# Decoder kernel on one core: the second cross attention's maxima are split behind their turning, and the expert layer's first weights are loaded and split under the attention's end

## Reference

```python
# layer 1 cross attention: 16 batches, 16 heads of 8 channels, 56 queries, 1500 keys
qh = _split_heads(q @ W_q.T + b_q, bs)
kh = _split_heads(k @ W_k.T + b_k, bs)
vh = _split_heads(v @ W_v.T + b_v, bs)
scores = jnp.einsum('bhqd,bhkd->bhqk', qh, kh) / jnp.sqrt(jnp.float32(D_K))
weight = jax.nn.softmax(scores, axis=-1)
attn = jnp.einsum('bhqk,bhkd->bqhd', weight, vh)
x = x + attn.reshape(...) @ W_o.T + b_o
# layer 1 experts: all 8 experts on all 896 tokens
gate = jax.nn.softmax(x @ Wg + bg, axis=-1)          # less a learned threshold, clipped, normalised
h = jax.nn.gelu(jnp.einsum('td,edf->etf', x, W1) + b1[:, None, :])
eo = jnp.einsum('etf,efd->etd', h, W2) + b2[:, None, :]
out = jnp.einsum('te,etd->td', w, eo)
```

## Time and profile before

| | |
|---|---|
| median of 3 runs | 1433.26 us (1430.25 to 1434.88) |
| profiled execution, its own time | 1429.79 us |
| its span in the trace | 1428.0 us |
| busy: PE / DVE / ACT / POOL | 1356.4 / 1065.1 / 864.0 / 767.4 us |

### The profile page before, as it was taken

One profiled execution on the slowest core, in us unless ns is written; L12 is line 12 of the kernel. 1 busy time (PEld: TensorE's weight loads), 2 busy tenths in 40 slices (PEclk: granted clock), 3 DMA queues, 4 the chain that ended last, 5 costly groups with the idle time before them and its releaser, 6 DMA issues.

```text
span 1428.0 us, 25410 instructions
## 1 busy us (share of the span) xinstructions
PE 1356.4 (95%) x9220; PEld 1012.2 (71%) x9220; DVE 1065.1 (75%) x2128; ACT 864.0 (61%) x1849; POOL 767.4 (54%) x431
## 2 busy tenths in 40 slices
PE   7889999999999999999998987899999999999898
PEld 4648888888888888888866754555556556555687
DVE  6458778888777887778844677677777777776787
ACT  4437667666667666667623553566666666665575
POOL 5026443334444444442260291588888888885363
PEclk9899999999999999999999999999999999999999
DMA  3132222211212222221150123446446446420331
GB/s 85 61 91 52 57 57 57 55 43 36 49 52 58 57 51 57 57 57 36 43 151 15 57 64 80 115 104 139 106 101 138 110 95 139 94 66 1 87 105 45
DMA packets 71803, 104.39 MB, mean 73 GB/s; under 512 B 14670, under 2 KB 54934, under 8 KB 71550
## 3 DMA queue, kind: packets, MB, share of 16 engines
q1 hardware_dynamic: 60062, 91.39, 25.6%
q10 hardware_dynamic: 11616, 11.38, 3.0%
HBM read 63.65 MB, written 2.11 MB: 46 GB/s over the span
## 4 chain that ended last, share of the span: by engine, by line
PE 79%; DVE 11%; DMA 3%; ACT 2%; issue 2%; SPq 1%; POOL 1%; ACTq 0%; DVEq 0%; POOLq 0%
PE PS L701 9%; PE PS L1104 6%; PE PS L715 6%; PE PS L689 5%; PE PS L690 5%; PE PS L691 5%; PE PS L1118 5%; PE PS L717 5%; PE PS L716 5%; PE PS L1084 5%; PE PS L1043 3%; PE PS L1049 3%; DMA inv_kept<-row_inv 2%; PE PS L744 2%; DVE QO_area L1399 2%
## 5 line engine op out<-in xcount | busy, mean ns | idle before, releaser
L1233 POOL TENSOR_TENSOR QO_area<-QO_area,prob_a 125x896 f32<-125x896 f32 x150 | 315.1, 2101 | 22.7 <-ACT prob_a L1325 3.2
L867 ACT ACTIVATE HL<-PS 125x512 fp32r<-125x512 f32 (+1 forms) x384 | 206.8, 539 | 177.8 <-PE PS L701 160.7
L959 DVE TENSOR_TENSOR HL<-PS,HL 125x512 fp32r<-125x512 f32 (+1 forms) x384 | 238.0, 622 | 74.6 <-ACT HL L867 53.5
L1399 DVE TENSOR_REDUCE QO_area<-PS 112x1 f32<-112x500 f32 x384 | 238.9, 670 | 60.3 <-PE PS L1084 60.2
L1325 ACT ACTIVATE prob_a<-PS 125x448 f32<-125x448 f32 x384 | 187.5, 540 | 103.9 <-PE PS L1104 100.5
L774 POOL TENSOR_TENSOR HL<-ctx_area,ones 125x512 fp32r<-125x512 f32 (+1 forms) x64 | 93.1, 1454 | 247.3 <-PE PS L717 189.3
L715 PE MATMUL PS<-HL 125*128 125x512 f32 (+1 forms) x384 | 155.7, 405 | 2.4 <-DVE HL L959 2.0
L689 PE MATMUL PS<-HL 128*128 128x500 f32 x336 | 153.1, 456 | 4.7 <-DVE HL L929 3.9
L1104 PEld LDWEIGHTS PS<-HL 98*125 98x125 f32 x768 | 102.9, 186 | 71.4 <-ACT prob_a L1325 37.9
L877 ACT ACTIVATE prob_a<-prob_a,neg_max 128x500 f32<-128x500 f32 x192 | 135.5, 706 | 26.7 <-DVE neg_max L951 25.4
L1084 PE MATMUL PS<-HL 96*112 96x500 f32 x384 | 129.4, 408 | 17.9 <-DVE QO_area L1399 15.3
(11 more groups left out here) (262 smaller groups left out, 2743.3 us busy)
## 6 DMA issues: line engine op xcount, KB each, us to landing
HL<-prob_b SPq DMA_DIRECT2D x128, 187.5 KB, 4.0
ctx_area<-in_ctx_T SPq DMA_DIRECT2D x16, 750.0 KB, 13.4
ctx_area<-in_ctx SPq DMA_DIRECT2D x16, 750.0 KB
HL<-ctx_area SPq DMA_DIRECT2D x64, 187.5 KB, 3.8
inv_area<-in_ctx_T SPq DMA_DIRECT2D x8, 750.0 KB, 4.1
prob_a<-in_ctx_T SPq DMA_DIRECT2D x8, 750.0 KB, 4.7
inv_area<-inv_kept ACTq DMA_DIRECT2D x16, 256.0 KB, 3.5
ctx_area<-in_L_ffn_W SPq DMA_DIRECT2D x16, 256.0 KB, 3.4
```

The costliest lines, as they stand in the source:

```text
L867: nc.scalar.activation(pH[k % 3][0:KC, 0:width(g)], PS[0:KC, 2 + k % 3, 0:width(g)], ACT.Copy)\
L959: nc.vector.tensor_tensor(pL[k % 3][0:KC, 0:width(g)], PS[0:KC, 2 + k % 3, 0:width(g)], pH[k % 3][0:KC, 0:width(g)].bitcast(fp32), ALU.sub ...
L1233: nc.gpsimd.tensor_tensor(late_acc[b % 2], before, late_p[n % LATE_P], ALU.add).then_inc(m["padd"], 1)
L1399: nc.vector.tensor_reduce(late_part[b % 2][:, u // NKB, u % NKB:u % NKB + 1], PS[0:2 * S, u % NKB, 0:KB], AX, ALU.max).then_inc(m["mx"], 1)
```

## The change

The maxima are turned over first, eight columns of plain fp32, and split afterwards: ScalarE's copy out of PSUM bank 7 rounds them to the high row, VectorE subtracts that from the same PSUM bank for the low row (`low_maxima`, signal `nmlow`). The turning and ScalarE's copy move from step 1 to step 0 of the batch; the low row's DMA is issued in step 1, behind a wait for `nmlow`. Batch b+2's first keys wait for `nmlow` in place of `nmcopy`.

In the expert layer SP's first loads wait for the last stack, and GpSimd's splitting waits for the last add of the probabilities, in place of the residual. The split weights get another place in `HL`: behind the first of the three key stacks, where the second was.

```diff
-        hl_taken = [0]
-        xn_hl = [halved(128, NTOK) for i in range(2)]
+        hl_taken = [4 * S2]
         w1_hl = [[halved(128, FF) for h in range(2)] for i in range(2)]
         w2_hl = [[halved(128, FF) for h in range(2)] for i in range(2)]
+        xn_hl = [halved(128, NTOK) for i in range(2)]
...
-        late_nmHL = [carve(2 * S, 16).bitcast(fp32r) for i in range(2)]
-        late_nmT = [carve(16, 2 * S).bitcast(fp32r) for i in range(2)]
+        late_nmT = [[carve(8, 2 * S).bitcast(fp32r) for r in range(2)] for i in range(2)]
...
                 if piece == 0:
                     if b >= 2:
-                        pe.wait_ge(m["nmcopy"], b - 1)
+                        pe.wait_ge(m["nmlow"], b - 1)
...
-                nc.tensor.transpose(PS[0:16, 7, 0:2 * S], late_nmHL[b % 2].bitcast(fp32),
+                nc.tensor.transpose(PS[0:8, 7, 0:2 * S], late_nm[b % 2],
                                     ident[0:2 * S, 0:2 * S]).then_inc(m["nmtr"], 1)
...
-                    if c == 1 and 0 <= b < B:
+                    if c == 0 and 0 <= b < B:
                         turn_maxima(b)
...
-                nc.scalar.activation(late_nmT[b % 2], PS[0:16, 7, 0:2 * S], ACT.Copy).then_inc(m["nmcopy"], 1)
+                nc.scalar.activation(late_nmT[b % 2][0], PS[0:8, 7, 0:2 * S], ACT.Copy).then_inc(m["nmcopy"], 1)
...
-                for r in range(2):
-                    act.dma_start(
-                        late_q[b % 3].bitcast(fp32)[3 * QUAD + r:3 * QUAD + r + 1, 0:HQ],
-                        late_nmT[b % 2].bitcast(fp32)[8 * r:8 * r + 8, :]).then_inc(m["nmrow"], 16)
+                send_maxima(b, 0)
+
+            def send_maxima(b, r):
+
+                if r:
+                    act.wait_ge(m["nmlow"], b + 1)
+                act.dma_start(
+                    late_q[b % 3].bitcast(fp32)[3 * QUAD + r:3 * QUAD + r + 1, 0:HQ],
+                    late_nmT[b % 2][r].bitcast(fp32)).then_inc(m["nmrow"], 16)
...
+                    if c == 0 and 0 <= b < B:
+                        place_maxima(b)
                     if c == 1 and 0 <= b < B:
-                        place_maxima(b)
+                        send_maxima(b, 1)
...
-                hl = late_nmHL[b % 2]
-                nc.vector.tensor_reduce(late_nm[b % 2], late_part[b % 2], AX, ALU.max, negate=True)
-                chain.link(dve, nc.vector.tensor_reduce(hl[:, 0:8], late_part[b % 2], AX, ALU.max, negate=True))
-                nc.vector.tensor_tensor(hl[:, 8:16], late_nm[b % 2], hl[:, 0:8].bitcast(fp32), ALU.subtract)\
+                nc.vector.tensor_reduce(late_nm[b % 2], late_part[b % 2], AX, ALU.max, negate=True)\
                     .then_inc(m["nmsplit"], 1)
+
+            def low_maxima(b):
+
+                dve.wait_ge(m["nmcopy"], b + 1)
+                if b >= 2:
+                    dve.wait_ge(m["nmrow"], 2 * 16 * (b - 1))
+                nc.vector.tensor_tensor(late_nmT[b % 2][1], PS[0:8, 7, 0:2 * S], late_nmT[b % 2][0].bitcast(fp32),
+                                        ALU.subtract).then_inc(m["nmlow"], 1)
...
+                    if c == 1 and 0 <= b < B:
+                        low_maxima(b)
...
         def experts_gpsimd(pool):
 
             m = ff
-            pool.wait_ge(x_ready, 5)
+            pool.wait_ge(la["padd"], (NC - 1) * B)
...
             sp.wait_ge(la["vmm"], 3 * B)
-            sp.wait_ge(x_ready, 5)
+            sp.wait_ge(la["stack"], 16 * 12 * B)
```

More of the change, by code:

```diff
@@ L284, in decoder_kernel @@
         ld_late = [sem(f"ld_late{i}") for i in range(2)]
-        names = ("wqrep qp qhi qlo q0set qset ones kmm khi klo stack vmm vev mxmm mx nmsplit nmtr nmcopy nmrow "
+        names = ("wqrep qp qhi qlo q0set qset ones kmm khi klo stack vmm vev mxmm mx nmsplit nmtr nmcopy nmlow nmrow "
                  "sc exp pv padd sum norm wo out").split()
```

## The result

| | before | after |
|---|---|---|
| median of 15 runs | 1433.26 us | 1421.33 us |
| lowest and highest | 1425.40 and 1439.89 | 1416.39 and 1425.07 |
| profiled execution, its own time | 1429.79 | 1423.68 |
| its span, mean granted clock | 1428.0, 0.984 | 1421.9, 0.976 |

The ratio is 0.9916, 95% interval 0.9897 to 0.9935: faster by 11.9 us, against a forecast of 9.7 and a predicted time of 1423.6. The two profiled executions are only 6.1 us apart, because the one of after ran at a lower clock (0.976) than most of its kernel's (mean 0.981), and the one of before at a higher one (0.984, against 0.981 over the 53 runs of its kernel whose clock is on record).

A forecast was written before the change was run, and what follows sets the result against it. TensorE held 79% of the chain, stalling 1.10 us a batch behind VectorE's maxima, which waited for GpSimd. Gains of 7.4 (attention) and 2.3 (experts) sum to -9.7: from the median 1433.26 to 1423.6 us, range 1415 to 1430.

The forecast's parts named there:

- The rule of who waits for GpSimd: VectorE's new subtraction, one input in PSUM and one in SBUF, should not wait for GpSimd's adds: 0.28 us.
- The rival in which the new subtraction waits: Late attention: subtraction waits for GpSimd as before, 1.84 instead of 0.28; +9.1 us, time 1442.4; chance 0.06.
- Part B: Expert layer: earlier weight loads and GpSimd splitting free VectorE's instructions and the turned gates; gain 2.3 us, bounds 0.2 and 4.3.
- The stall, and what is late next: Late attention, step 1: TensorE's 1.10 us stall goes, 0.42 returns as wait for ScalarE, 0.68 gained in 12 batches.
- The rival of no new wait: Late attention: TensorE gets the whole 1.10 us per batch; 12.4 + 2.3, time 1417.6; chance 0.18.
- No cost on `nmlow`, without margin: TensorE's first keys wait for `nmlow`, due at 1004.55; TensorE gets there about 1004.6, so no cost.
- a sign of being wrong: Named signs: the batch period stays, `nmlow` shows as a wait of TensorE, or the layer norm grows.
- The low row's landing: Rival that the low row's DMA lands late for the batch's first scores; about 2 us fits the lead; no chance given.
- Batches 0 and 1, 0.8 lost: First two batches have no stall to lose and get the new wait, 0.4 us each.
- From batch 13 on the adds set the end: GpSimd adds for batches 13 and 14 back to back, so the turnings of batches 14 and 15 give nothing.
- my upper bound: Expert layer: if TensorE's clock stays at 2.4 GHz, the gain there is 4.3 us instead of 2.3.
- The cast: Expert layer: VectorE's cast, 0.85 us, may or may not have waited for GpSimd's instruction; 0 to 0.37.

The follow-up runs named there:

- experiment 3: Changed kernel, but ScalarE also copies the turned maxima unrounded to SBUF and VectorE's subtraction takes both inputs from SBUF; 1436.89 us, ratio 1.0028 to before.
- experiment 4: Changed kernel, but ScalarE issues the low row's DMA in step 2, behind the keys' high part; 1419.21 us, ratio 0.9899 to before.
- Part B alone: Kernel before, with only the expert layer's early loads, early splitting and new place of the split weights; 1426.0 us, ratio 0.9965 to before.
- Experiment 6: Changed kernel plus two unused TensorE products of 128 columns ahead of each step from batch 15's scores on; 1419.89 us, ratio 0.9914 to before.
- experiment 5: Changed kernel, but GpSimd's splitting waits for the normalised tokens, so runs under VectorE's gates again, loads still early; 1422.43 us, ratio 0.9928 to before.
- experiment 1: Changed kernel with both expert-layer waits (SP's loads, GpSimd's splitting) back on the last residual; 1424.07 us, ratio 0.9949 to before.
- experiment 7: Changed kernel, but VectorE takes batch 14's last four adds from GpSimd; 1422.94 us, ratio 0.9944 to before.
- the late DMA: Changed kernel with the low row's DMA issued behind step 2's keys, measured twice: 1419.21 us (ratio 0.9899) and 1418.25 us (0.9893).

## Why the prediction was right, and where its sizes were off

**The rule of who waits for GpSimd** carried the forecast and holds: 0.25 in 16 of 16 batches with one operand in PSUM, up to 2.18 with both in SBUF. The rival in which the new subtraction waits did not happen, and experiment 3 shows what it would have given: not +9.1 but +4 by the ratio of 1.0028, with Part B in it, as in my sum, and a second copy on ScalarE besides. I had priced it at the old 1.84; at its new place it met the adds at other moments, median 1.18.

**The stall, and what is late next.** Stall 1.10, net gain 0.68, return through ScalarE 0.42: measured 0.79 and 0.38. The steps came as forecast, TensorE 1.82 and 1.65 (1.75 and 1.65), the exponential 1.57 behind its scores (1.4). I was 0.1 a batch low, in pieces of 0.03: subtraction 0.25 for 0.28, issue 0.63 for 0.66, and the rest of the chain. Over 12 batches that is 1.3 us of the 2.2 that I was short. The rival of no new wait falls with `ACT prob_a L1324: 17.1`, and its sum is what experiment 4 gives back. TensorE's second keys waited 0.37 for VectorE, where I had said about 0.7.

**No cost on `nmlow`, without margin:** it showed as a wait of TensorE once, 0.6. I had named any such wait as a sign of being wrong; it came, too small to matter. In experiment 3, where the subtraction is late, the same wait comes 14 times, 13.2 in all.

**The low row's landing.** I took some 2 us for it from the Trainium skill ("DMA: Bandwidth & Descriptors"), whose figure stands in "Anatomy of one DMA — SWDGE (gpsimd) path", so for a DMA issued from GpSimd. This one is ScalarE's; experiment 4 measured 1.78 from the start of its issue. It fits inside the lead, as I had said.

**Batches 0 and 1, 0.8 lost.** Measured 1.51, but little of it is the change. The first keys start at 897.56, before 897.22, 0.34 later (forecast 0.4). In batch 1 the maxima stand at 922.22 and the keys at 929.15, 6.93; before 920.92 and 927.64, 6.72: 0.21. The other 0.96 goes with the clock: over the ten experiments batch 1's first add moves with the granted clock of 900 to 910, from 938.36 at 0.51 over 933.16 at 0.74 to 928.65 at 1.00. At 0.63 stand both after (934.98) and Part B alone (935.35), whose first batches do the old work. (Experiment 6, with the change in it, stands at 932.18 at 0.82, before at 933.47 at 0.81.) So the 0.8 may be 0.55 or nothing; one trace can't price it.

**From batch 13 on the adds set the end.** Right: from batch 13's first add to GpSimd's last end it is 49.12 before and 49.11 after.

**What I did not see** is what lies behind them. I took the last batch for fixed, and it lost 5.1 in the profiled execution. Before, TensorE came to the row sums when GpSimd's last add was done; with the shorter periods it comes 1.45 ahead of it, and I did not price what the clock may do after such a wait. My sum had the last batch at nothing. Beside the periods it is the largest term in the trace; it is in four of the five traces with that wait, and in how many of the 15 runs is not known.

**Part B, 2.3.** Measured 3.16, in the three pieces that I had named. The first hidden product came 1334.71 - 1325.58 = 9.13 behind the layer norm's start and comes 1330.60 - 1322.64 = 7.96: 1.17 (forecast 1.1). The wait of 1.47 at the turned gates is gone, since L1958 and L1966 take 0.28 and 0.37 instead of 1.08 and 1.19. And TensorE does the same 24 products in 1337.36 - 1330.60 = 6.76 instead of 1342.59 - 1334.71 = 7.88, another 1.12, because the clock is back at 1.00 from 1335 on the earlier trace rows; this was my upper bound (clock stays up, 4.3), of which about half came in this trace. Together 3.76 at the turned gates, of which 0.6 is lost later. The layer norm did not grow: its reciprocals take 1.56 beside the splitting as without.

How much of this is the clock, the other traces tell. All nine with the early splitting lie between 98.8 and 100.5 from the layer norm to the end: 98.8 to 99.3 where the clock was low for about 3 us around the first hidden products (six traces), 100.1 to 100.5 where it was low for about 7 (three). The three with GpSimd under the gates take 102.4, 103.1 and 104.2, all with about 7 us in all. So at about the same clock Part B gives at least 1.9 (102.4 against the 100.5 of Part B alone), and the rest of the 3.16 comes in those executions in which the clock is back early. My 2.3 lies between.

**The cast,** 0 to 0.37 by the rows: it took 0.63 against 0.85, 0.22. The Trainium skill ("SBUF — State Buffer", Who interferes with whom) has whichever of the two engines comes second wait for the other's whole instruction where a cast runs in a two-port mode; the traces agree, with the cast's end 0.49 and 0.48 behind GpSimd's where GpSimd was first, and GpSimd's instruction the longer one where the cast was (experiment 5), and put the price at 0.22 here and 0.58 in experiment 1.

**The median.** Without the last batch's fall and with 0 to 0.55 for the first batches the account is 9.55 + 3.16 - 0.55 = 12.2 to 12.7; the runs give 12.0 at equal clock and 11.9 between the medians. The comparison at equal clock takes the price of a fall out (and Part B's share of the clock with it), so it may be held against this account, roughly. The medians do not: over the five traces with the wait the last batch loses 3.4 on average, and with that the account would be 8.7 to 9.3. Some 3 us between the medians stay open; the clocks of the 15 runs of before are not on record. Counted without the fall I was 2.2 short: 1.3 from the periods, 0.9 from the experts. That the time came so near the forecast is in part luck: the gain was larger than I had it, and what the last batch can lose was missing from the sum.

## What to carry to other kernels

When a short instruction on VectorE stretches beside GpSimd, see whether one of its operands can be read from PSUM before looking for another place for it; the place alone gave at most 0.1 of 0.79 us a batch here. Before moving work to another engine's queue, see what stands behind it there: in experiment 7 an add that waited 4.84 us held up a subtraction of 0.26, and through it two more engines. A DMA issued on a compute engine's queue stands between its exponentials for 0.63 us plus the wait ahead of it: put it behind the work that somebody needs. Before pricing terms of a microsecond from one trace, compare traces of the same code: where the granted clock falls in some executions and not in others, only runs, or stretches at the same clock, can tell.

## What the runs showed of the hardware

The mean granted clock of one unchanged kernel lay between 0.971 and 0.985 over twelve runs (the late DMA), and its time between 1411.0 and 1425.2, more than the change under study had to give in either of its parts. The same kernel had the fall to 1.2 GHz behind the same wait in one trace (24.6 us for the last batch) and not in another (19.5); over five traces with that wait the clock was low for 0 to 21 us behind it. In both traces with independent products in the last batch the clock stayed up, at a sure cost of 2.6 us against a possible one of 5.1. And ScalarE's row named GpSimd as the releaser of a wait that went away when a DMA issue was moved.
